# Sparse expert stages in 71 blocks and three phases instead of 78 blocks and two parts, with the prologue's ring copies moved ahead of a root

## Chip, cores and metric

The kernel runs on one core of one Trainium2 chip. The metric is the time of one execution on the device, in microseconds (us); the median of several runs is compared.

## What is computed

The reference is a network of four layers on an input of 8 x 32 x 32 tokens with 64 channels; each layer adds a mixing step (a cosine transform, a convolution, a hyperbolic convolution, a spherical transform) and a feed-forward step to its input, each on normalised rows. The feed-forward steps of the last two layers, called ffn2 and ffn3 in the kernel, are mixtures of 8 experts of which each token takes the best two:

```python
flat = x.reshape(-1, C)                      # 8192 tokens, C = 64, normalised
logits = flat @ router_w.T                   # 8 experts
probs = jax.nn.softmax(logits, axis=-1)
topk_probs, topk_idx = jax.lax.top_k(probs, TOP_K)          # TOP_K = 2
topk_probs = topk_probs / (jnp.sum(topk_probs, axis=-1, keepdims=True) + 1e-09)
gates = jnp.einsum('nk,nke->ne', topk_probs, onehot)
h = jax.nn.silu(einsum('nc,ehc->neh', flat, w1)) * einsum('nc,ehc->neh', flat, w3)   # hidden 682
y = jnp.einsum('neh,ech->nec', h, w2)
out = jnp.einsum('ne,nec->nc', gates, y)
```

## The kernel before

The network's eight stages run one after the other with a barrier between them. The change concerns the two calls of `sparse_stage` (ffn2 and ffn3). The 8192 tokens lie as 64 tiles of 128. Only the two chosen experts are computed for a token: its row is copied to a slot of its expert in DRAM, slots are worked on in blocks of 256 rows of one expert, and results go back to the token's place.

A sparse stage has two programs with a barrier between. The **prologue** normalises the rows in four pieces (`PARTS`: tiles 0 to 7, 8 to 15, 16 to 39, 40 to 63). VectorE centres, sums the squares and scales (`centre`, `variance`, `scale`), ScalarE squares and takes the root (`square`, `take_root`, L1079). TensorE turns the scaled rows (L1033, PSUM tile turn_ps), ScalarE copies them to the tile ring (`keep`, L1088), TensorE multiplies by the router (L1044). VectorE then chooses the two experts (`choose`, from L898), takes the gates, and computes each row's slot (`place`) in two ranges, tiles 0 to 15 and 16 to 63. A first range of 16 tiles lets GpSimd begin early: it stores each tile's rows twice, once per choice, by an indirect DMA (`store_row`, L821), 32 stores in the prologue. `table` (L947 to L970) makes for each range the list of blocks: which expert, which place. SP clears the unfilled end of each expert's region with zero rows (L1019), whose source tile pads VectorE clears (L992).

The **loop** runs over 78 blocks: 23 for the first range and 55 for the second, each 2 x rows / 256 plus 7 spare ones, since each expert's rows of a range begin a block of their own. For each block SP loads the block's 256 rows (x, `load_x`, L1182, 66 KB) and its expert's weights (`load_weights`, L1189, 534 KB), each from a place held in a register; every 13 blocks it loads the registers anew (L1171). Weights have 4 buffers and wait for the down-projection of four blocks earlier; x is issued two blocks ahead of its weights (`X_LEAD`). TensorE turns x (`turn_x`, L1234), ScalarE copies it (L1293), and three pairs of hidden chunks follow: TensorE's up-projection (L1245, 8 matmuls a pair, 24 a block), ScalarE's SiLU (L1303), VectorE's product (L1333). TensorE's order in a block is: up-projection of pairs 0 and 1, turn x of the next block, fold the block before the last, pair 2, down-projection (L1256) of the block before. The trace joins pair 2's successors where they stand together, so a row of 16 up-projection matmuls is the start of a block. VectorE multiplies by the gate (L1321), GpSimd stores the results by two indirect DMAs a block (L1224). Ahead of these stand, on GpSimd, the 96 row stores of the second range. The x of block 23 waits for all of them:

```python
if b == BLOCKS[0]:
    sp.wait_ge(row_stored[1], 16 * 2 * (TILES - SPLIT))
    sp.wait_ge(pads_stored[1], 16 * E)
```

In the **tail** the results are loaded back (L1214), each token's two, and added to X (L1346): tiles 0 to 15 are loaded while the last 13 blocks run, tiles 16 to 63 after the last store, in six pieces of 8 tiles with two loads each.

## Time and profile before

| | |
|---|---|
| three runs | 2366.31, 2366.70, 2370.96 us, median 2366.7 |
| the profiled execution | 2369.53 us, its span 2367.7 us |
| busy in the span | TensorE 74%, VectorE 54%, ScalarE 42%, GpSimd 26% |
| mean granted TensorE clock | 0.842 of 2.4 GHz |
| up-projection matmuls of ffn2 and ffn3 (L1245) | 3744, 491.6 us |
| ffn2: stage start to the loop's start, to the last addition | 1193, 1274, 1712 us |
| ffn3: the loop's start, the last addition | 1919, 2360 us |

A page of the profile shows busy time by engine and in 40 slices of the span, the DMA queues, the chain of work that ended last, and the costliest groups of instructions. A timeline row gives the start in us from the span's start, the duration in us, the engine, the line of the kernel, the operation, what it writes and reads, a count where equal neighbours are joined, and in brackets how long the engine stood idle before it and what ended that. SPq is SP's queue, where only its DMA issues show. The names PE, DVE, ACT and POOL stand for TensorE, VectorE, ScalarE and GpSimd.

### The profile page before, as it was taken

The numbers are of one execution on the slowest core, as the hardware profiler recorded it, in microseconds if no ns is written. First come the engines' busy times: TensorE is split into PE (matmuls) and PEld (weight loads), VectorE is DVE, ScalarE is ACT, GpSimd is POOL, SyncE is SP. The second block draws the span as 40 slices with busy tenths as digits, with TensorE's granted clock in tenths as the row PEclk, the third lists the DMA queues.
The fourth block names the chain that finished last, engine by engine and source line by source line (L and its number), as shares of the span: only waits on it lengthen the run. The fifth ranks groups of instructions, "written<-read, shape, count | busy, mean of one in ns | idle before, by whom it ended". The sixth has DMA issues, their size and how long they took to land. (4 is left out here: it accounts for less than half of the span.)

```text
span 2367.7 us, 31990 instructions
## 1 busy us (share of the span) xinstructions
PE 1756.1 (74%) x11745; PEld 1022.3 (43%) x11745; DVE 1283.6 (54%) x2424; ACT 1000.0 (42%) x1785; POOL 619.5 (26%) x619
## 2 busy tenths in 40 slices
PE   2899996879999942111234999999566449999995
PEld 1633333336333331000022666666356326666663
DVE  6553336665433367688775545555561755455554
ACT  2466653334656532352222444444233324444442
POOL 0100000001000000000035777433351457773332
PEclk8699997996999955555556999999888579999997
DMA  1222210001222100000012544444365134444453
GB/s 49 62 67 63 67 50 20 0 19 55 66 64 70 45 13 0 0 0 0 0 39 85 151 143 142 141 129 156 105 124 110 42 105 143 136 146 134 133 152 133
DMA packets 125790, 187.03 MB, mean 79 GB/s; under 512 B 39194, under 2 KB 73242, under 8 KB 125122
## 3 DMA queue, kind: packets, MB, share of 16 engines
q1 hardware_dynamic: 107458, 166.08, 24.6%
q0 software_dynamic: 18176, 18.91, 2.4%
q8 instruction: 94, 1.54, 0.3%
q14 instruction: 62, 0.51, 0.1%
HBM read 157.26 MB, written 27.65 MB: 78 GB/s over the span
## 5 line engine op out<-in xcount | busy, mean ns | idle before, releaser
L1333 DVE TENSOR_TENSOR ffn_hidden<-ffn_silu,ffn_up_ps 114x512 f32<-114x512 f32 x468 | 321.9, 688 | 397.5 <-ACT ffn_silu L1303 396.6
L1245 PE MATMUL ffn_up_ps<-ffn_turned,ffn_weights 64*114 64x256 f32 x3744 | 491.6, 395 | 20.9 <-DMA ffn_weights<-in_ffn_weights 13.9
L1303 ACT ACTIVATE ffn_silu<-ffn_up_ps 114x512 f32<-114x512 f32 x468 | 279.5, 597 | 445.1 <-PE ffn_up_ps L1245 442.7
L821 POOL DMA_INDIRECT slots<-ffn_rows,ffn_slot x256 | 253.5, 990 | 550.1 <-DVE ffn_slot L938 384.3
L736 ACT ACTIVATE ffn_hidden<-ffn_up_ps,ffn_b 128x512 f32<-128x512 f32 x512 | 310.3, 689 | 198.5 <-PE ffn_up_ps L631 198.5
L1224 POOL DMA_INDIRECT results<-ffn_yout,ffn_xin x312 | 300.4, 963 | 306.3 <-DVE ffn_yout L1321 239.0
L1245 PEld LDWEIGHTS ffn_up_ps<-ffn_turned,ffn_weights 64*114 64x114 f32 x3744 | 318.0, 176 | 136.3 <-issue 80.2
L631 PE MATMUL ffn_up_ps<-ffn_T,ffn_up_w 64*128 64x512 f32 x1024 | 264.5, 630 | 2.2 <-ACT ffn_hidden L736 2.2
L652 PE MATMUL ffn_y_ps<-ffn_hidden,ffn_down 128*64 128x512 f32 x1024 | 247.8, 605 | 2.5 <-DVE ffn_y_total L526 2.5
L1256 PE MATMUL ffn_y_ps<-ffn_hidden,ffn_weights 114*64 114x256 f32 x1872 | 236.4, 388 | 0.0
L526 DVE SCALAR_TENSOR_TENSOR ffn_gated<-ffn_y_ps,ffn_b,ffn_gates 128x512 f32<-128x512 f32 x96 | 72.0, 751 | 204.7 <-PE ffn_y_ps L652 203.1
L631 PEld LDWEIGHTS ffn_up_ps<-ffn_T,ffn_up_w 64*128 64x128 f32 x1024 | 92.9, 190 | 168.8 <-ACT ffn_hidden L736 92.2
L1256 PEld LDWEIGHTS ffn_y_ps<-ffn_hidden,ffn_weights 114*64 114x64 f32 x1872 | 120.5, 136 | 98.8 <-DVE ffn_hidden L1333 52.7
L652 PEld LDWEIGHTS ffn_y_ps<-ffn_hidden,ffn_down 128*64 128x64 f32 x1024 | 62.4, 136 | 160.7 <-ACT ffn_hidden L736 84.4
L1234 PE MATMUL ffn_x_ps<-ident,ffn_xin 128*64 128x128 f32 x312 | 64.6, 289 | 34.2 <-DMA ffn_xin<-slots 34.2
L1267 PE MATMUL ffn_out_ps<-fold,ffn_y_half 128*128 128x64 f32 x624 | 87.8, 264 | 1.4 <-DVE ffn_y_half L1314 1.4
L526 DVE SCALAR_TENSOR_TENSOR ffn_y_total<-ffn_y_ps,ffn_b,ffn_gates 128x512 f32<-128x512 f32 x32 | 23.7, 750 | 115.1 <-PE ffn_y_ps L652 92.0
L1267 PEld LDWEIGHTS ffn_out_ps<-fold,ffn_y_half 128*128 128x128 f32 x624 | 82.4, 192 | 3.2 <-DVE ffn_y_half L1314 1.7
L1033 PE MATMUL ffn_turn_ps<-ident,D 128*128 128x128 f32 x64 | 17.3, 431 | 87.5 <-DVE D L874 87.5
L1314 DVE COPY ffn_y_half<-ffn_y_ps 128x256 f32<-128x256 f32 x156 | 66.3, 425 | 19.8
L1948 POOL MEMSET dc_first<- 128x128 f32 x1 | 0.2, 204 | 288.7 <-POOLq L3081 288.7
L2709 POOL MEMSET hyp_ones<- 128x128 f32 x1 | 0.2, 204 | 288.3 <-POOLq L3081 288.3
(402 smaller groups left out, 2144.7 us busy)
## 6 DMA issues: line engine op xcount, KB each, us to landing
ffn_weights<-in_ffn_weights SPq DMA_DIRECT2D x156, 534.0 KB
ffn_gates<-gate_rows SPq DMA_DIRECT2D x128, 256.0 KB
ffn_xin<-slots SPq DMA_DIRECT2D x156, 66.0 KB, 3.2
sht_mix<-in_sht_weights SPq DMA_DIRECT2D x8, 1024.0 KB, 8.2
results<-ffn_yout,ffn_xin POOLq DMA_INDIRECT x312
slots<-ffn_rows,ffn_slot POOLq DMA_INDIRECT x256
D<-results SPq DMA_DIRECT2D x12, 256.0 KB, 4.8
ffn_second<-results SPq DMA_DIRECT2D x12, 256.0 KB, 5.6
```

What stands on the lines that cost most here:

```text
L526: nc.vector.scalar_tensor_tensor(target, y_ps[th][:, :], b2[:, p:p + 1], gates[:, n % GATES, th, :], ALU.add, ALU.mult).then_inc(y_gated, 1)
L631: nc.tensor.matmul(up_ps[j][:, :], up_w[rows, 2 * p + half, c * P:(c + 1) * P], T[rows, g * NTOK:(g + 1) * NTOK], start=True, stop=True).t ...
L652: last = nc.tensor.matmul(y_ps[th][rows, :], down[:, 2 * p + half, c, :], hidden[:, n % 2 * UNITS + 2 * half + th, :], start=(c == 0), sto ...
L736: nc.scalar.activation(hidden[:, n % 2 * UNITS + j, :], up_ps[j][:, :], ACT.Gelu, bias=b1[:, bias_at:bias_at + 1], scale=1.0).then_inc(hid ...
L821: nc.gpsimd.indirect_dma_start(k.slots, bass.IndirectOffsetOnAxis(slot[c][:, t:t + 1], 0), rows[c][:, t, :], None).then_inc(row_stored[h], 16)
L1224: nc.gpsimd.indirect_dma_start(k.results, bass.IndirectOffsetOnAxis(xin[:, b % HELD, j, CH + 1:CH + 2].bitcast(I32), 0), yout[:, b % HELD, ...
L1245: last = nc.tensor.matmul(up_ps[w][n % 2][0:SIZE, chunk % 2 * BLOCK:(chunk % 2 + 1) * BLOCK], weights[rows_of, b % WEIGHTS, chunk * SIZE:( ...
L1256: last = nc.tensor.matmul(y_ps[b % 2][half * CH:(half + 1) * CH, 0:BLOCK], weights[0:SIZE, b % WEIGHTS, col:col + CH], hidden[0:SIZE, b % ...
L1267: last = nc.tensor.matmul(out_ps[:, j * CH:(j + 1) * CH], y_half[:, b % 2, j * P:(j + 1) * P], k.fold[:, :], start=True, stop=True)
L1303: nc.scalar.activation(silu[0:SIZE, n % 2, :], up_ps[0][n % 2][0:SIZE, :], ACT.Silu).then_inc(silu_done, 1)
L1314: nc.vector.tensor_copy(y_half[:, b % 2, :], y_ps[b % 2][:, 0:BLOCK]).then_inc(y_kept, 1)
L1333: nc.vector.tensor_tensor(hidden[0:SIZE, b % 2, c, :], silu[0:SIZE, n % 2, :], up_ps[1][n % 2][0:SIZE, :], ALU.mult).then_inc(hidden_done, 1)
```

## The change

The second range is split once more for the loop: the blocks come in three phases, 9, 16 and 46, together 71. `LANDED` gives the tiles whose rows must be stored before a phase: 0 to 15, 16 to 31, 32 to 63. Each expert now has one region for all its rows. In the first two phases only blocks that are already full are taken (a count of whole blocks, cut off at 9 and at 16), and the last phase takes all that is left, so that only one partly filled block remains per expert. For this `table` runs three times, keeps a count of the blocks taken (`passed`), and has 17 or 18 operations instead of 13. Unfilled ends are cleared once, after `place(1)`, with a pads tile of half the width. GpSimd's stores are in the same order with two semaphores instead of one. x of a block is issued right behind its weights (only x of block 0 ahead). In the prologue ScalarE's ring copies of the third piece stand ahead of the root of the fourth, and VectorE clears pads behind the scaling of the fourth piece. In the tail all 64 tiles are loaded after the last store, in eight pieces.

```diff
+LANDED = ((0, SPLIT), (SPLIT, 2 * SPLIT), (2 * SPLIT, TILES))
-BLOCKS = tuple(2 * (t1 - t0) * P // BLOCK + SPARES for t0, t1 in RANGES)
+FULL = tuple(2 * t1 * P // BLOCK - SPARES for _, t1 in LANDED[:-1])
+ALL_SLOTS = 2 * TOKENS // BLOCK + SPARES
+PHASES = (FULL[0], FULL[1] - FULL[0], ALL_SLOTS - FULL[1])
+PHASE_AT = (0, FULL[0], FULL[1])
-PADS = 2 * E + 2 * SPARES
+PADS = E + SPARES
...
                 def table(i):
                     ch.link(nc.vector.tensor_reduce(r.blocks[:, :], short, AX.X, ALU.add))
+                    ch.link(nc.vector.tensor_tensor(r.blocks[:, :], r.blocks[:, :], r.passed[:, 0:E], ALU.subtract))
...
+                    ch.link(nc.vector.tensor_scalar(r.starts[:, 1:E + 1], r.starts[:, 1:E + 1], float(nb), None,
+                                                    ALU.min))
+                    ch.link(nc.vector.tensor_tensor(r.taken[:, :], r.starts[:, 1:E + 1], r.starts[:, 0:E],
+                                                    ALU.subtract))
...
                 centre(3)
+                variance(3)
+                scale(3)
                 ch.link(nc.vector.memset(pads[:, :, :, :], 0.0))
                 ch.link(nc.vector.tensor_copy(pads[:, :, :, CH + 1].bitcast(I32), pad_dest), "pads")
-                variance(3)
-                scale(3)
                 table(0)
                 choose(1)
                 gates(1)
                 place(1)
                 table(1)
+                table(2)
...
                 square(3)
+                keep(2)
                 take_root(3)
-                keep(2)
                 keep(3)
...
-            TAIL = 6
+            TAIL = 8
...
                 def load_x(place, b):
                     if b >= HELD:
                         sp.wait_ge(y_stored[b % HELD], 2 * 16 * (b // HELD))
-                    if b == BLOCKS[0]:
-                        sp.wait_ge(row_stored[1], 16 * 2 * (TILES - SPLIT))
-                        sp.wait_ge(pads_stored[1], 16 * E)
+                    if b in PHASE_AT:
+                        i = PHASE_AT.index(b)
+                        sp.wait_ge(row_stored[i], 16 * 2 * (LANDED[i][1] - LANDED[i][0]))
+                    if b == PHASE_AT[-1]:
+                        sp.wait_ge(pads_stored, 16 * E)
+                        sp.wait_ge(spares_stored, 16)
...
-                for b, place in enumerate(registers(block_place, 0, X_LEAD)):
-                    load_x(place, b)
                 for first in range(0, SLOT_BLOCKS, TURN):
-                    experts = registers(block_expert, first, TURN)
-                    places = registers(block_place, first + X_LEAD, min(TURN, SLOT_BLOCKS - first - X_LEAD))
-                    for b in range(first, first + TURN):
+                    count = min(TURN, SLOT_BLOCKS - first)
+                    places, experts = registers(block_place, first, count), registers(block_expert, first, count)
+                    for b in range(first, first + count):
+                        if b == 0:
+                            load_x(places[0], 0)
                         load_weights(experts[b - first], b)
-                        if b + X_LEAD < SLOT_BLOCKS:
-                            load_x(places[b - first], b + X_LEAD)
-                    if first + TURN == SLOT_BLOCKS - TURN:
-                        for b in range(BLOCKS[0]):
-                            sp.wait_ge(y_stored[b], 2 * 16)
-                        for c in (0, 1):
-                            sp.dma_start(back_to[c][:, 0:SPLIT, :], back[c][:, 0:SPLIT, :]).then_inc(first_back, 16)
+                        if b > 0:
+                            load_x(places[b - first], b)
...
-                for t in range(*RANGES[1]):
-                    for c in (0, 1):
-                        store_row(1, c, t)
+                for i in (1, 2):
+                    for t in range(*LANDED[i]):
+                        for c in (0, 1):
+                            store_row(i, c, t)
```

ScalarE in the prologue, from the square of tiles 16 to 39 to the copies of the scaled rows. Before:

```order
L1074 ACTIVATE ffn_second<-D 128x1536
L1079 ACT_TABLE_LOAD
L1079 ACTIVATE ffn_root<-ffn_var,eps_t 128x24
L1074 ACTIVATE ffn_second<-D 128x1536
L1079 ACTIVATE ffn_root<-ffn_var,eps_t 128x24
L1088 COPY ffn_ring<-ffn_turn_ps 128x512 x6
L1094 COPY ffn_rows<-D 128x24x64 x4
```

Now:

```order
L1098 ACTIVATE ffn_second<-D 128x1536
L1103 ACT_TABLE_LOAD
L1103 ACTIVATE ffn_root<-ffn_var,eps_t 128x24
L1098 ACTIVATE ffn_second<-D 128x1536
L1112 COPY ffn_ring<-ffn_turn_ps 128x512 x3
L1103 ACTIVATE ffn_root<-ffn_var,eps_t 128x24
L1112 COPY ffn_ring<-ffn_turn_ps 128x512 x3
L1118 COPY ffn_rows<-D 128x24x64 x4
```

Three of the six ring copies now stand between the second square and the second root.

SP at the start of the loop, from the first register load (TENSOR_LOAD) to the first weights; an ISA row prepares the issue behind it. Before:

```order
L1171 TENSOR_LOAD ffn_block_place
L1182 ISA
L1182 DMA ffn_xin<-slots 128x132
L1182 ISA
L1182 DMA ffn_xin<-slots 128x132
L1171 TENSOR_LOAD ffn_block_expert
L1171 TENSOR_LOAD ffn_block_place
L1189 ISA
L1189 DMA ffn_weights<-in_ffn_weights 128x1068
```

Now, to the x of block 1:

```order
L1192 TENSOR_LOAD ffn_block_place
L1192 TENSOR_LOAD ffn_block_expert
L1206 ISA
L1206 DMA ffn_xin<-slots 128x132
L1213 ISA
L1213 DMA ffn_weights<-in_ffn_weights 128x1068
L1213 ISA
L1213 DMA ffn_weights<-in_ffn_weights 128x1068
L1206 ISA
L1206 DMA ffn_xin<-slots 128x132
```

Both register loads stand first, x of block 0 is the only one ahead of weights, and x of block 1 stands behind the weights of block 1.

VectorE in the prologue, the third and fourth piece between `place(0)` and the first table. Before:

```order
L874 TENSOR_TENSOR D<-D,ffn_rstd 128x1536
L860 TENSOR_REDUCE ffn_mean<-X 128x24
L861 SCALAR_TENSOR_TENSOR D<-ffn_mean,X 128x1536
L992 MEMSET ffn_pads 128x3960
L993 CAST ffn_pads<-ffn_consts 128x60
L868 TENSOR_REDUCE ffn_var<-ffn_second 128x24
L873 RECIPROCAL ffn_rstd<-ffn_root 128x24
L874 TENSOR_TENSOR D<-D,ffn_rstd 128x1536
L947 TENSOR_SCALAR ffn_count<-ffn_count 128x8
L948 TENSOR_TENSOR ffn_wide<-ffn_consts,ffn_count 128x64
```

Now:

```order
L865 TENSOR_REDUCE ffn_mean<-X 128x24
L866 SCALAR_TENSOR_TENSOR D<-ffn_mean,X 128x1536
L873 TENSOR_REDUCE ffn_var<-ffn_second 128x24
L878 RECIPROCAL ffn_rstd<-ffn_root 128x24
L879 TENSOR_TENSOR D<-D,ffn_rstd 128x1536
L1020 MEMSET ffn_pads 128x1980
L1021 CAST ffn_pads<-ffn_consts 128x30
L960 TENSOR_SCALAR ffn_counts<-ffn_counts 128x8
L961 TENSOR_TENSOR ffn_wide<-ffn_consts,ffn_counts 128x64
L965 TENSOR_REDUCE ffn_blocks<-ffn_wide 128x8
```

The clearing of pads, 1980 columns instead of 3960, now stands behind the scaling of D and ahead of the first table.

## Rows read from the trace of the kernel before

**Rows 1.** TensorE, loop of ffn2: start us, us, engine line op out<-in xcount [idle].

```profile
1302.95 0.41 PE L1234 MATMUL ffn_x_ps<-ident,ffn_xin 128*64 128x128 f32 x2
...
1401.32 1.99 PE L1245 MATMUL ffn_up_ps<-ffn_turned,ffn_weights 64*114 64x256 f32 x16 [2.43 <-issue]
...
1684.37 1.99 PE L1245 MATMUL ffn_up_ps<-ffn_turned,ffn_weights 64*114 64x256 f32 x16
```

**Rows 2.** Stretches: us, busy of PE, PEld, DVE, ACT, POOL, PEclk, DMA share, GB/s.

```profile
2041.00:2054.00 13.00, 9.24 (x56) 6.16 (x54) 3.72 (x7) 2.72 (x6) 9.95 (x11) 0.74 0.51 173
1404.00:1684.00 280.00, 280.00 (x2287) 187.47 (x2288) 146.39 (x273) 131.05 (x273) 136.47 (x143) 1.00 0.44 139
1703.00:1708.00 5.00, 0.00 (x0) 0.00 (x0) 3.84 (x6) 0.00 (x0) 0.00 (x0) 0.50 0.95 332
```

**Rows 3.** TensorE's timeline, the pause in ffn3's loop.

```profile
2045.80 3.76 PE L1245 MATMUL ffn_up_ps<-ffn_turned,ffn_weights 64*114 64x256 f32 x16 [3.76 <-issue]
...
2053.63 1.99 PE L1245 MATMUL ffn_up_ps<-ffn_turned,ffn_weights 64*114 64x256 f32 x16
```

**Rows 4.** SP's queue, loads in the loops of ffn2 and ffn3.

```profile
1296.65 0.33 SPq L1182 DMA_DIRECT2D ffn_xin<-slots  x1
...
1344.47 0.50 SPq L1182 DMA_DIRECT2D ffn_xin<-slots  x1
...
1397.09 0.33 SPq L1182 DMA_DIRECT2D ffn_xin<-slots  x1
...
1944.95 0.40 SPq L1182 DMA_DIRECT2D ffn_xin<-slots  x1
...
2041.68 0.33 SPq L1182 DMA_DIRECT2D ffn_xin<-slots  x1
```

**Rows 5.** VectorE's timeline, prologue of ffn2.

```profile
1226.36 3.36 DVE L992 MEMSET ffn_pads<- 128x3960 f32 x1 [0.89 <-DVE D L861]
...
1234.48 0.17 DVE L947 TENSOR_SCALAR ffn_count<-ffn_count 128x8 f32<-128x8 f32 x1
...
1247.89 0.75 DVE L898 COPY ffn_L<-ffn_small_ps 128x192 f32<-128x192 f32 x2 [9.59 <-PE ffn_small_ps L1044]
...
1268.08 0.17 DVE L947 TENSOR_SCALAR ffn_count<-ffn_count 128x8 f32<-128x8 f32 x1
...
1273.40 0.19 DVE L970 CAST ffn_block_place<-ffn_place_f 128x55 int32<-128x55 f32 x1
```

**Rows 6.** SP's queue, then TensorE's timeline, start of ffn2's loop.

```profile
1274.80 0.91 SPq L1182 DMA_DIRECT2D ffn_xin<-slots  x2
1279.71 0.34 SPq L1189 DMA_DIRECT2D ffn_weights<-in_ffn_weights  x1
...
1284.38 3.76 PE L1245 MATMUL ffn_up_ps<-ffn_turned,ffn_weights 64*114 64x256 f32 x16 [7.05 <-DMA ffn_weights<-in_ffn_weights]
```

**Rows 7.** VectorE's timeline, ffn2's tail; then the chain that ended last, ffn3's.

```profile
1711.55 0.69 DVE L1346 TENSOR_TENSOR X<-X,ffn_second 128x512 f32<-128x512 f32 x1
...
2351.74 6.35 DMA ffn_second<-results
```

**Rows 8.** GpSimd's timeline, ffn2: the loop's 32nd row store.

```profile
1313.91 0.96 POOL L821 DMA_INDIRECT slots<-ffn_rows,ffn_slot  x1 [0.31 <-issue]
```

**Rows 9.** Loads of the input tile in ffn2, all 78: time to landing.

```profile
DMA to landing us min/median/max: 3.0/3.2/3.8
```

**Rows 10.** ScalarE's, then TensorE's timeline, prologue of ffn2.

```profile
1225.51 1.48 ACT L1074 ACTIVATE ffn_second<-D 128x1536 f32<-128x1536 f32 x1 [5.81 <-DVE D L861]
1231.93 0.31 ACT L1079 ACTIVATE ffn_root<-ffn_var,eps_t 128x24 f32<-128x24 f32 x1 [4.94 <-DVE ffn_var L868]
1232.15 1.05 ACT L1088 COPY ffn_ring<-ffn_turn_ps 128x512 f32<-128x512 f32 x2
1235.73 0.59 ACT L1088 COPY ffn_ring<-ffn_turn_ps 128x512 f32<-128x512 f32 x1 [2.53 <-PE ffn_turn_ps L1033]
...
1237.44 1.11 PE L1033 MATMUL ffn_turn_ps<-ident,D 128*128 128x128 f32 x4
```

122 lines of the change are left out of this document (62 added, 60 removed).

## The prediction

> **What bounds the kernel now.** From the page (the table above) I took only that TensorE leads and where its clock is full. Then I read its timeline inside a block loop. From block 22 to block 77 of ffn2 the up-projections of one block start one period after those of the block before: (1684.37 - 1401.32) / 55 = 5.146 us [rows 1], and over 1404 to 1684 us TensorE is busy in all of the 280 us at granted clock 1.00, the 2.4 GHz level [rows 2]. So in the loop a block costs what TensorE needs for it, and a block less is 5.146 us less. The weights are read anew for each block and no instruction depends on how full a block is, so an empty block costs the same.
>
> Three places around that loop are not TensorE's. First, block 22: its up-projections start 2.43 us late in ffn2 [rows 1], and 3.76 us late in ffn3 [rows 3]. SP's queue says why: x of block 23, the first of the second part, is issued in front of the weights of block 22, and SP issues it only at 1397.09 (ffn3: 2041.68) [rows 4], when GpSimd has stored the rows of all 48 remaining tiles. In ffn3 the first 16 matmuls after the pause take 3.76 instead of 1.99 us, and the granted clock is 0.74 over 2041 to 2054, part of it at the 1.2 GHz level [rows 2]: block 22 lasts 2053.63 - 2045.80 = 7.83 us, 2.7 more than a period. The wait costs 2.4 us in ffn2 and 3.8 + 2.7 = 6.4 us in ffn3. Second, the start: VectorE ends the last table at 1273.6 [rows 5], SP issues its first load at 1274.80 and the first weights at 1279.71, and TensorE's first up-projection, held by those weights, comes 4.67 us later [rows 6]. Third, the tail: after the last block the results of tiles 16 to 63 come back and are added pair by pair until 1712.2 [rows 7].
>
> **The change, part by part.** The durations are those of the profiled execution, 2369.5 us (span 2367.7); the median of the three runs, 2366.7, lies 2.8 us lower, and the sum is put on the median at the end.
>
> *Blocks.* 78 becomes 71 in each stage: 7 x 5.146 = 36.0 us, twice: -72.0 us. They come off the full-clock part, where no other engine could have hidden them.
>
> *The wait at block 22.* It goes, and two later waits could take its place: x of block 9 wants the rows of tiles 16 to 31, x of block 25 those of tiles 32 to 63. Each now stands behind the weights of its own block. The slot behind the weights of block 4 is 1296.65 and then one per period [rows 4], so x of block 9 is due at 1322.4 and of block 25 at 1404.7. GpSimd's stores come 0.96 + 0.30 = 1.26 us apart, and the 32nd of the loop starts at 1313.91 [rows 8]; 64 stores before SP's release at 1397.09 is 1316.4, 2.5 us after that start. So the rows are there 6.0 and 7.6 us early. In ffn3 the slot of block 5 is 1944.95 [rows 4]: 1965.5 against 2041.68 - 80.6 = 1961.1, and 2047.9 against 2041.7, so 4.4 and 6.2 us. Loop and stores start from the same barrier; SP's earlier start (below) takes 0.9 us off each margin, which leaves at least 3.5 us. Behind such a wait on SP stand the weights of the next block, due a period later, and TensorE stops only if x comes over 3 us too late on top (next edit). So neither wait stops TensorE: -2.4 - 6.4 = -8.8 us; bounds: nothing gained if the wait only moves, and all of it.
>
> *Input loads.* x was issued two blocks ahead; now x of block b follows the weights of block b, which wait for the down-projection of block b - 4. The old slot behind the weights of block 4 is 1296.65 [rows 4], and TensorE turns the rows of block 4 at 1302.95 [rows 1]: 6.3 us. x lands 3.0 to 3.8 us after its issue in all 78 loads of ffn2 [rows 9], nearly all of them issued right behind a weight load, as now. That leaves 2.5 us. At every 13th block SP reloads its registers: the slot due at 1296.65 + 9 x 5.146 = 1342.96 came at 1344.47 [rows 4], 1.5 us late, and there 1.0 us is left. Cost nothing; bounds nothing and about 10 us (ten such blocks by 1 us).
>
> *Prologue.* On ScalarE the three ring copies of tiles 16 to 39 move ahead of the root of tiles 40 to 63. They waited behind that root until 1232.15; now they start when the square ends, at 1227.0, and the third, 3.6 us after the first as before, ends at 1231.2. The root starts there instead of at 1231.93, the scaling ends 2.55 us later as before, at 1233.7 instead of 1234.5, and TensorE's next transposes, which stood at 1237.44 behind the late copies, start at once [rows 5, 10]. The steps after them run as before, so the router's logits come 3.7 us earlier and VectorE's second choice starts at 1244.2 instead of 1247.89. The clearing of the padding moves behind that scaling at half the width, half of 3.36 us; with the first table it ends near 1240, inside VectorE's wait of 9.59 us before that choice [rows 5]. Without that cover it would cost its 1.7 us.
> Against this stand the tables. The old one behind the choice took 1268.08 to 1273.59, 5.5 us for 13 operations of 8 to 440 columns; the old first one, from 1234.48 until that wait began at 1238.30, 3.8 us for 13 of 8 to 184 [rows 5]. Now two follow the choice: 18 operations of 8 to 128 columns, at most 3.8 + 5 x 0.2 = 4.8, and 17 of 8 to 368, about 5.1 + 4 x 0.2 = 5.9 (a small operation is 0.17 us, about 0.2 with the step to the next); with one more small operation 10.9 us. That is 5.4 more, minus the 3.7: the loop may begin 1.7 us later. SP gives some back: the load of x of block 1 and a short register load, 0.9 us together by my estimate from the two loads' 0.91 us at 1274.80 and the 1.2 us before it [rows 5, 6], no longer stand ahead of the first weights; x of block 0 now runs beside those weights (66 KB, 0.2 us at the 332 GB/s below). Net +1.0 us a stage, +2.0; bounds -1 and +4 a stage.
>
> *Tail.* The first 16 tiles came back early; now 8 pairs of 256 KB loads instead of 6 follow the last store. VectorE's two additions of a pair, 0.69 us each [rows 7], are 2.8 us for two more pairs if the data is there; 2 x 0.52 MB at the 332 GB/s of 1703 to 1708 us, with the DMA engines 0.95 busy, are 3.2 us [rows 2]. In ffn3 the chain ends on a transfer that took 6.35 us [rows 7], so there the DMA decides. I take 3.0 us a stage, +6.0; bounds 2.4 (a quarter faster transfers) and 6 a stage.
> The Trainium skill (DMA: Bandwidth & Descriptors, Specifications) gives a fabric ceiling of 435 GB/s; at that the extra 1.05 MB would be an estimated 2.4 us a stage, hidden by VectorE's additions, and the sum 0.4 us lower. The row with engines 0.95 busy at 332 GB/s does not bear that out for these transfers.
>
> Sum: -72.0 - 8.8 + 2.0 + 6.0 = -72.8 us. On the profiled execution that is 2296.7, on the median 2366.7 - 72.8 = 2293.9, say **2294 us**.
>
> **The rivals.**
> *The wait moves.* The new boundaries wait as the old one did. For it: the margin of block 9 in ffn3 is 3.5 us, and if GpSimd is slowed, all 32 stores grow. Against it: the pitch of 1.26 us fits the 64 stores after the 32nd as well. TensorE would stop once the 32 stores took 6 us (15%) longer. Each wait then costs 2.4 to 6.4 us as before, two to four of them: 2299 to 2320, most likely two by 5, 2304.
> *Reload blocks wait.* x misses its turn at the ten blocks after a register reload, by 1 us each: 2304.
> *The lead is too short everywhere* (the other side). If x, now just in time, landed later than 6.3 us after its issue, each block would wait: every 0.1 us costs 142 x 0.1 = 14 us, and from 6.8 us on the change is slower than before; at 7.0 us it would stand at 2294 + 99 = 2393. Against it: none of 78 took over 3.8 us beside weights and stores.
> *The blocks were free.* If the seven blocks cost nothing, being spare ones without rows, only -8.8 + 8.0 remains, 2366. Against it: 55 periods in a row of one length, the last ones among them.
>
> **How the numbers follow.** 0.84 for the forecast, 0.08 for the moved wait, 0.05 for the reload blocks, 0.02 for the short lead, 0.01 for free blocks. 0.2% (4.7 us) is about what a measurement of this kernel can tell from no change. Faster: 0.84 + 0.08 + 0.05 = 0.97; same 0.01; slower 0.02. Range: downwards the prologue's bound gives 4 and the tail's 1.2, and the runs shown scatter by 2 about their middle: 2287. Upwards the bounds of prologue and tail give 6 each: 2306, and 1 for the rest; that takes in most of the two middle rivals: 2307.
>
> **What would show it.** 24 x 142 = 3408 up-projection matmuls; period 5.15; no pause over 1 us in the loops and clock 1.00 throughout them once it has risen; SP's x of blocks 9 and 25 right behind the weights; VectorE's second choice 3.7 us earlier and its last table 1.7 us later than now, against the stage's start; from the last result store to the last addition 3 us more. A period above 5.2, or pauses at blocks 9, 25, 13 or 26, would make me wrong.

## The result, and the profile after

The changed kernel takes 2288.97 us (median of four executions, 2279.4 to 2290.99) where the kernel before, on the same chip, took 2366.51: a ratio of 0.966, 95% interval 0.9631 to 0.969. Repeated on another occasion it was 2286.04 against 2368.84, ratio 0.9645 (0.9618 to 0.9672). The forecast was 2294, range 2287 to 2307. The direction and the bulk are right; the gain is larger than forecast (-77.5 us, in the repetition -82.8, where -72.8 was predicted), and 0.966 x 2366.7 = 2286.2 us lies below the range.

The profiled execution of the changed kernel is the 2279.4 one (span 2277.6), 9.6 us under its median. So the two spans, 90.1 us apart, may not be compared as wholes: 10 us of it lie in the first dense stage, which the change does not touch (last section). I compare the two sparse stages piece by piece, each piece from a start inside the stage. The stage starts are SP's first issue of the router weights: 1193.05 and 1838.88 us before, 1186.64 and 1790.15 after. The last piece ends at SP's first issue of the next stage, in ffn3 at its issue of the network's output.

| us | forecast, ffn2 / ffn3 | ffn2: before, after, difference | ffn3: before, after, difference |
|---|---|---|---|
| stage start to first up-projection | +1.0 / +1.0 | 91.33, 89.55, **-1.78** | 89.85, 88.67, **-1.18** |
| first up-projection to start of last result store | -38.4 / -42.4 | 412.41, 372.82, **-39.59** | 415.22, 371.99, **-43.23** |
| start of last result store to next stage's start | +3.0 / +3.0 | 16.99, 19.70, **+2.71** | 17.11, 20.10, **+2.99** |
| sum | -34.4 / -38.4 | -38.66 | -41.42 |

The sparse stages together gave -80.1 instead of -72.8: of the 7.3 us more, 5.0 are in the first row and 2.0 in the second. The tail is right within 0.3. In the repetition's profile the same pieces, against the same profile before, give -78.4: 5.6 us more than forecast, 4.7 of them in the first row and 0.9 in the second, with the tail right within 0.1. So the first row's miss repeats; of the second row's, half is no more than two profiles of one kernel differ by.

The loop first. The page's row of the up-projections and the stretches of both loops after the clock has risen:

```profile
L1262 PE MATMUL ffn_up_ps<-ffn_turned,ffn_weights 64*114 64x256 f32 x3408 | 445.8, 394 | 5.8 <-DMA ffn_weights<-in_ffn_weights 4.9
```

```profile
1290.00:1640.00 350.00, 350.00 (x2858) 234.25 (x2857) 182.90 (x340) 163.62 (x341) 206.80 (x216) 1.00 0.46 139
1892.00:2240.00 348.00, 348.00 (x2842) 232.88 (x2844) 182.13 (x339) 162.29 (x338) 206.82 (x217) 1.00 0.46 139
```

3408 matmuls instead of 3744, as counted, TensorE busy in every microsecond at granted clock 1.00, the 2.4 GHz level; the last column and the one before are GB/s and DMA share, 139 as before [rows 2] and 0.46 for 0.44. The pause that stood in [rows 1, 3] is nowhere: each gating multiplication of VectorE follows the one before by 5.14 or 5.15 us in both stages, but for the last two gaps, which are shorter. SP's queue in ffn2 shows why the new boundaries don't wait, with GpSimd's 32nd and 96th row store of the loop beside it:

```profile
1313.44 0.33 SPq L1213 DMA_DIRECT2D ffn_weights<-in_ffn_weights  x1
1313.96 0.33 SPq L1206 DMA_DIRECT2D ffn_xin<-slots  x1
...
1395.79 0.33 SPq L1213 DMA_DIRECT2D ffn_weights<-in_ffn_weights  x1
1396.37 0.33 SPq L1206 DMA_DIRECT2D ffn_xin<-slots  x1
```

```profile
1308.90 0.96 POOL L826 DMA_INDIRECT slots<-ffn_rows,ffn_slot  x1 [0.31 <-issue]
...
1389.72 0.95 POOL L826 DMA_INDIRECT slots<-ffn_rows,ffn_slot  x1 [0.30 <-issue]
```

Before, SP issued x of block 23 2.37 us after the start of the 96th store (to 1397.09 [rows 4]):

```profile
1394.72 0.95 POOL L821 DMA_INDIRECT slots<-ffn_rows,ffn_slot  x1 [0.30 <-issue]
```

By that, the rows of block 9 are there at 1308.90 + 2.37 = 1311.3 and those of block 25 at 1392.1: 2.7 and 4.3 us before their loads, which stand 0.5 us behind the weights like every other. The same reckoning gives 2.0 and 3.6 us in ffn3.

Now the first row of the table. VectorE's prologue in ffn2, after:

```profile
1220.53 1.75 DVE L873 TENSOR_REDUCE ffn_var<-ffn_second 128x24 f32<-128x1536 f32 x1 [1.62 <-ACT ffn_second L1098]
...
1227.39 1.71 DVE L1020 MEMSET ffn_pads<- 128x1980 f32 x1 [0.48 <-DVE D L879]
...
1237.42 0.75 DVE L903 COPY ffn_L<-ffn_small_ps 128x192 f32<-128x192 f32 x2 [3.81 <-PE ffn_small_ps L1068]
...
1257.86 0.17 DVE L960 TENSOR_SCALAR ffn_counts<-ffn_counts 128x8 f32<-128x8 f32 x1
...
1268.42 0.19 DVE L992 CAST ffn_block_place<-ffn_place_f 128x46 int32<-128x46 f32 x1
```

Against its stage's start the second choice (the copy of the logits) stood at 1247.89 - 1193.05 = 54.84 us [rows 5] and stands at 50.78: 4.06 earlier, 3.7 forecast. The two tables behind the choice take 1268.61 - 1257.86 = 10.75, forecast 10.9. So the last table ends 81.97 us after the start instead of 80.54: +1.43, forecast +1.7. Up to here the sum holds. It breaks in SP's queue:

```profile
1271.24 0.37 SPq L1206 DMA_DIRECT2D ffn_xin<-slots  x1
1271.79 0.88 SPq L1213 DMA_DIRECT2D ffn_weights<-in_ffn_weights  x2
```

```profile
L1192 SPq TENSOR_LOAD <-ffn_block_place x1: 987/987/987, 1269.1 to 1269.1; - x1
L1192 SPq TENSOR_LOAD <-ffn_block_expert x1: 964/964/964, 1270.1 to 1270.1; - x1
```

From the end of the last table to the first weights it was 1279.71 - 1273.59 = 6.12 us [rows 5, 6] and is 1271.79 - 1268.61 = 3.18: 2.94 less (ffn3: 2.96), where I had taken 0.9. The second pair of lines (loads of the table into SP's registers: ns shortest/median/longest, and their start) shows two loads of 13 registers in about 1.0 us each. The same view of the kernel before, at the same place, has three: 476 ns for two registers, 1023 for the 13 experts, and 2731 for 13 places.

```profile
L1171 SPq TENSOR_LOAD <-ffn_block_place x2: 476/1604/2731, 1274.2 to 1276.8; - x2
L1171 SPq TENSOR_LOAD <-ffn_block_expert x1: 1023/1023/1023, 1275.8 to 1275.8; - x1
```

TensorE's first up-projection follows the first weights by 4.40 us, where it was 4.67 [rows 6]:

```profile
1276.19 3.76 PE L1262 MATMUL ffn_up_ps<-ffn_turned,ffn_weights 64*114 64x256 f32 x16 [2.48 <-DMA ffn_weights<-in_ffn_weights]
```

And the second row: it is -36.0 for the blocks and -2.4 (ffn2) for the pause, and 1.2 more (ffn3: 0.8 more). Before, one of the last four result stores takes 1.79 us instead of 0.96 (GpSimd's and VectorE's timeline, end of ffn2 before; then GpSimd's after):

```profile
1693.17 1.22 DVE L1346 TENSOR_TENSOR X<-X,D 128x1024 f32<-128x1024 f32 x1
1693.42 1.79 POOL L1224 DMA_INDIRECT results<-ffn_yout,ffn_xin  x1 [0.31 <-issue]
1694.42 1.23 DVE L1346 TENSOR_TENSOR X<-X,ffn_second 128x1024 f32<-128x1024 f32 x1
...
1695.52 0.96 POOL L1224 DMA_INDIRECT results<-ffn_yout,ffn_xin  x1 [0.30 <-issue]
```

```profile
1646.48 0.96 POOL L1241 DMA_INDIRECT results<-ffn_yout,ffn_xin  x1 [0.30 <-issue]
1647.74 0.96 POOL L1241 DMA_INDIRECT results<-ffn_yout,ffn_xin  x1 [0.30 <-issue]
1649.01 0.96 POOL L1241 DMA_INDIRECT results<-ffn_yout,ffn_xin  x1 [0.30 <-issue]
```

The long store of before starts while VectorE makes the early addition of tiles 0 to 15, and ends 0.82 us after the end of that addition's first operation. Without the early addition none of these stores is long. Those 0.83 us a stage were not in my sum.

The tail. The chain that ended last, in ffn3 after:

```profile
2254.78 5.10 DMA ffn_second<-results
2260.63 1.31 DVE X L1363 x2
```

Behind that transfer VectorE's additions follow one another to the end; before, the chain went through a transfer of 6.35 us instead [rows 7]. So the tail is now bound by the additions: four more of 0.69 us, 2.8 us, where I had let the transfers' 3.2 us decide and taken 3.0.

### The profile page after: what moved, and what is told of

The parts are those of the page before. It is cut to its first block and busy times, and to the rows that moved or that the text cites. A ratio compares the mean times of both kernels' runs of the same rounds, so it can differ in the third digit from the quotient of the medians.

```text
span 2277.6 us, 30440 instructions
## 1 busy us (share of the span) xinstructions
PE 1677.3 (74%) x11157; PEld 967.5 (42%) x11157; DVE 1245.0 (55%) x2416; ACT 965.8 (42%) x1715; POOL 590.1 (26%) x591
## 5 line engine op out<-in xcount | busy, mean ns | idle before, releaser
L1350 DVE TENSOR_TENSOR ffn_hidden<-ffn_silu,ffn_up_ps 114x512 f32<-114x512 f32 x426 | 293.0, 688 | 349.9 <-ACT ffn_silu L1320 349.0
L1262 PE MATMUL ffn_up_ps<-ffn_turned,ffn_weights 64*114 64x256 f32 x3408 | 445.8, 394 | 5.8 <-DMA ffn_weights<-in_ffn_weights 4.9
L1320 ACT ACTIVATE ffn_silu<-ffn_up_ps 114x512 f32<-114x512 f32 x426 | 254.4, 597 | 388.9 <-PE ffn_up_ps L1262 386.5
L1241 POOL DMA_INDIRECT results<-ffn_yout,ffn_xin x284 | 271.9, 957 | 246.0 <-DVE ffn_yout L1338 179.6
L1262 PEld LDWEIGHTS ffn_up_ps<-ffn_turned,ffn_weights 64*114 64x114 f32 x3408 | 288.1, 176 | 110.6 <-issue 59.6
L1273 PE MATMUL ffn_y_ps<-ffn_hidden,ffn_weights 114*64 114x256 f32 x1704 | 215.2, 388 | 0.0
L1273 PEld LDWEIGHTS ffn_y_ps<-ffn_hidden,ffn_weights 114*64 114x64 f32 x1704 | 109.7, 136 | 89.9 <-DVE ffn_hidden L1350 48.2
L1284 PE MATMUL ffn_out_ps<-fold,ffn_y_half 128*128 128x64 f32 x568 | 79.7, 263 | 1.4 <-DVE ffn_y_half L1331 1.4
L2138 PE MATMUL dc_conv_ps<-dc_fresh,dc_step_w 128*128 128x512 f32 x144 | 67.6, 617 | 8.8 <-DVE dc_fresh L2124 8.8
L1310 ACT COPY ffn_turned<-ffn_x_ps 64x256 f32<-64x256 f32 x142 | 50.1, 353 | 56.0 <-PE ffn_x_ps L1251 56.0
```

Source lines behind the costliest of these rows:

```text
L1241: nc.gpsimd.indirect_dma_start(k.results, bass.IndirectOffsetOnAxis(xin[:, b % HELD, j, CH + 1:CH + 2].bitcast(I32), 0), yout[:, b % HELD, ...
L1262: last = nc.tensor.matmul(up_ps[w][n % 2][0:SIZE, chunk % 2 * BLOCK:(chunk % 2 + 1) * BLOCK], weights[rows_of, b % WEIGHTS, chunk * SIZE:( ...
L1273: last = nc.tensor.matmul(y_ps[b % 2][half * CH:(half + 1) * CH, 0:BLOCK], weights[0:SIZE, b % WEIGHTS, col:col + CH], hidden[0:SIZE, b % ...
L1284: last = nc.tensor.matmul(out_ps[:, j * CH:(j + 1) * CH], y_half[:, b % 2, j * P:(j + 1) * P], k.fold[:, :], start=True, stop=True)
L1320: nc.scalar.activation(silu[0:SIZE, n % 2, :], up_ps[0][n % 2][0:SIZE, :], ACT.Silu).then_inc(silu_done, 1)
L1350: nc.vector.tensor_tensor(hidden[0:SIZE, b % 2, c, :], silu[0:SIZE, n % 2, :], up_ps[1][n % 2][0:SIZE, :], ALU.mult).then_inc(hidden_done, 1)
```

## The experiments

Two theories stood for the 5 us of the prologue: that a register load is quick or slow by **where its first entry lies** (every slow one of both traces starts at an entry that is no multiple of four, that is not on 16 bytes, every quick one of 13 on one: before, places from entry 2, 15 and 41 took 2.7, from entry 28 0.98), or by **what was issued ahead of it** (before, two row transfers). Two runs set one against the other.

Six of the runs of this section are single executions: the old table moved, the new tables moved, the early addition moved, both orders undone, cleared twice, and the kernel before with the copies ahead. Their whole times tell little, and what is read from them lies inside a stage.

**The old table moved to 16 bytes.**

```
-block_place = sb("block_place", [P, SLOT_BLOCKS], I32)
+block_place = sb("block_place", [P, SLOT_BLOCKS + 2], I32)   # entries from column 2 on
-registers(block_place, first + X_LEAD, ...)
+registers(block_place, first + X_LEAD + 2, ...)
```

> The kernel before, with one edit: the table of block places lies two entries further in its tile, so that the load of places 2 to 14 into SP's registers begins at a multiple of four entries (16 bytes) instead of at entry 2. Same loads, same transfers, same order. Theory (a register load is quick, 75 ns a register, where its first entry lies on 16 bytes, and slow, 205 ns a register, elsewhere): that load at the start of each sparse stage's loop takes 1.0 us instead of 2.73, the first weights are issued 1.75 us earlier, and each stage is 1.75 us shorter, 3.5 in all; the later loads of places turn quick where they start at entries 15, 28, 41 ... plus 2 = 4 entries' multiples and slow elsewhere. Rival (the load is slow because two transfers of rows were issued just ahead of it, or because of where its instructions lie): it stays at 2.7 us and no stage changes.

The load takes 989 ns, with the two row transfers still ahead of it:

```profile
L1172 SPq TENSOR_LOAD <-ffn_block_place x1: 989/989/989, 1278.2 to 1278.2; - x1
```

The first up-projection comes 89.01 and 87.86 us after the stage's start instead of 91.33 and 89.85: 2.3 and 2.0 earlier. But the stages did not get shorter (start to last addition 521.9 and 519.9 us; before 519.2 and 520.7), and the time is 2368.71 us beside 2369.51. The second half of the expectation is a miss. TensorE's timeline in ffn2's loop shows where the two microseconds went, and more:

```profile
1403.30 3.76 PE L1246 MATMUL ffn_up_ps<-ffn_turned,ffn_weights 64*114 64x256 f32 x16 [5.93 <-issue]
```

Block 22 now waits 5.93 us where it waited 2.43 [rows 1], in ffn3 6.31 where it waited 3.76 [rows 3]. GpSimd's stores did not start sooner, and in both stages SP issues x of block 23 2.37 us after the 96th of them, as before. Part of the growth is scatter: in the run with the moved addition (below), whose start is that of the kernel before, the two pauses are 4.41 and 2.12 us. But there too the pause is long where the loop was early: in ffn2 the first gating multiplication came 104.40 us after the stage's start, where it was 106.11 before and is 103.25 here; in ffn3 105.54, 103.42 and 101.42. Pause and start add up to 108.5 to 109.2 us in ffn2 and 107.2 to 107.7 in ffn3 in all three traces. Whatever the loop gains at its start, that pause takes back; and behind a long pause the first matmuls take 3.76 instead of 1.99 us, as in [rows 3]. So in the kernel before, the quick load is worth nothing; it is worth its 2 us only together with the pause's removal.

**The new tables moved off 16 bytes.**

```
-mine = slice(PHASE_AT[i], PHASE_AT[i] + nb)
+mine = slice(PHASE_AT[i] + 1, PHASE_AT[i] + nb + 1)
-table[0:1, bass.ds(first, count)]
+table[0:1, bass.ds(first + 1, count)]
```

> The changed kernel, with one edit: both block tables lie one entry further in their tiles, so that SP's two first loads of 13 registers begin at entry 1 instead of entry 0. Theory (a load whose first entry is not on 16 bytes takes 205 ns a register instead of 75): both take 2.7 us instead of 0.98 and 0.96, the first weights come 3.4 us later after VectorE's last table, and since no wait further on takes it up, each sparse stage ends 3.4 us later, 6.9 in all: the old kernel's slow start is back. Of the later loads, begun at entries 14, 27, 40, 53 and 66, none is quick (in the changed kernel the pair at entry 52 was). Rival (the changed kernel's first loads are quick because no transfer was issued ahead of them): they stay below 1.1 us.

```profile
L1192 SPq TENSOR_LOAD <-ffn_block_place x1: 2732/2732/2732, 1276.2 to 1276.2; - x1
L1192 SPq TENSOR_LOAD <-ffn_block_expert x1: 2698/2698/2698, 1278.9 to 1278.9; - x1
...
L1192 SPq TENSOR_LOAD <-ffn_block_place x1: 1052/1052/1052, 1474.5 to 1474.5; - x1
L1192 SPq TENSOR_LOAD <-ffn_block_expert x1: 968/968/968, 1475.6 to 1475.6; - x1
```

Both first loads are slow again, with no transfer ahead of them. I had written that no later load would be quick; the pair at 1474.5 is, and it starts at entry 39 + 1 = 40, a multiple of four that I had overlooked. The rule, not my list, was right. The first up-projection comes 93.84 and 91.56 us after the start; in the unedited kernel of the repetition 89.50 and 88.99: 4.3 and 2.6 later, 6.9 together. The two stages are 5.5 us longer to their last addition (485.2 and 481.8 against 481.1 and 480.4), and the time is 2293.64 us beside 2363.43.

**The lead of the rows taken away in the kernel before.**

```
-for b, place in enumerate(registers(block_place, 0, X_LEAD)):
-    load_x(place, b)
...
+if b == 0: load_x(places[0], 0)
 load_weights(experts[b - first], b)
-if b + X_LEAD < SLOT_BLOCKS: load_x(places[b - first], b + X_LEAD)
+if b > 0: load_x(places[b - first], b)
```

> The kernel before, with one edit: the lead of the rows over the weights is taken away, so that the rows of a block are asked for right behind its weights (rows of block 0 ahead of them), as in the changed kernel. 78 blocks, two phases, and the early add stay. Theory: the row transfer that waits for the second phase's stores (block 23) now stands two weight loads further back, 10.3 us later, so the pause of TensorE at block 22 goes in both stages (2.4 and 6.4 us); the place table's first load starts at entry 0 and takes 1.0 us instead of 0.48 + 2.73, so the first weights come some 2 to 2.9 us earlier a stage; in all -8.8 and -4 to -6, 2352 to 2354 us against 2366.5. Rival 1 (the pause was bound to the number of stores, not to the lead): a pause of 2 us or more remains at block 22 or 23 and the time is over 2358. Rival 2 (rows asked for so late are late at every block): the period of 5.146 us grows, and the time is above 2366.

2358.05 us against 2369.51, ratio 0.9958 (0.9944 to 0.9972): 9.9 us less by the ratio and 11.5 by the medians, where 13 to 15 were expected. The register loads behaved (0.98 and 0.97 us), the first up-projection came 2.9 and 2.1 us earlier, and the period stayed 5.146, so rows asked for right behind the weights are not late; only once, behind a reload of the registers in ffn3, did TensorE wait for rows (0.39 us). But the pause did not go, it shrank to about 1.5 us in each stage. It now stands at the transposes of block 23's rows, with SP's row ahead of it:

```profile
1398.50 0.33 SPq L1181 DMA_DIRECT2D ffn_xin<-slots  x1
```

```profile
1400.47 0.41 PE L1233 MATMUL ffn_x_ps<-ident,ffn_xin 128*64 128x128 f32 x2 [1.42 <-DMA ffn_xin<-slots]
```

So the smaller lead was not the whole cure: what freed the changed kernel is that and the boundary, which moved from block 23 to 25, 10.3 us later on TensorE, for the same 96 stores. Rival 1 is half right.

**The early addition moved behind the first tail transfer, in the kernel before.**

```
-dve.wait_ge(first_back, 32)
-add(0, SPLIT)
 for i, (t0, t1) in enumerate(tail):
     dve.wait_ge(tail_back[i], 32)
+    if i == 0: dve.wait_ge(first_back, 32); add(0, SPLIT)
     add(t0, t1)
```

> The kernel before, with one edit: the adds of tiles 0 to 15 wait for the first tail transfer, so they no longer run beside the last four result stores. Everything is still computed. Theory (the add of two SBUF operands on VectorE holds up GpSimd's store beside it): all of the last four stores of each sparse stage take 0.96 us, none 1.79, and the last store comes 0.83 us earlier after its up-projections than before; the two adds (1.2 us each) then lie in VectorE's idle time between the tail pieces, so each stage is about 0.8 us shorter, 1.7 in all. Rival (the long store is late for another reason, its own transfer queue for example): one store of 1.79 us stays, and nothing is earlier. Second rival: the adds push the tail's own adds back, and a stage becomes up to 2.5 - 0.8 = 1.7 us longer although the store is short.

```profile
1694.22 0.96 POOL L1224 DMA_INDIRECT results<-ffn_yout,ffn_xin  x1 [0.30 <-issue]
1695.48 0.96 POOL L1224 DMA_INDIRECT results<-ffn_yout,ffn_xin  x1 [0.30 <-issue]
1696.75 0.96 POOL L1224 DMA_INDIRECT results<-ffn_yout,ffn_xin  x1 [0.30 <-issue]
```

In both stages all of the last stores are short. So the addition beside it is what made one long. Three stores of ffn2's prologue before begin within an operation of VectorE of 1.76 us on two operands in SBUF, and each ends 0.83 us after that operation does. The longest of them:

```profile
1232.68 1.76 DVE L874 TENSOR_TENSOR D<-D,ffn_rstd 128x1536 f32<-128x1536 f32 x1
1232.91 2.36 POOL L821 DMA_INDIRECT slots<-ffn_rows,ffn_slot  x1 [0.30 <-issue]
```

The additions did not fit in idle time, though: from the last store to the last addition it is 16.7 and 16.9 us instead of 15.5 and 15.6, so the stage loses 1.2 and gains 0.83: the second rival, smaller than its bound. The whole, 2368.34 beside 2369.51, tells nothing here.

The Trainium skill (SBUF — State Buffer, "SBUF: two separate sides") says that a VectorE operation with two SBUF inputs and a GpSimd operation that reads SBUF exclude each other for a whole instruction. That fits the rows of 1.79 and 2.36 us for the stores, which end 0.82 and 0.83 us after VectorE's operation, much as if they had only begun there. The trace does not show it for VectorE: its next operation on two SBUF operands starts at 1694.42 and takes its usual 1.23 us beside the rest of the store. The prediction did not draw on this page.

**The prologue's two moves.** Three edits of the changed kernel and one of the kernel before price them; the measure is the second choice's distance from the stage's start in ffn2 (54.84 before, 50.78 after, 50.79 in the repetition).

```
 keep(2) / take_root(3)      ->  take_root(3) / keep(2)                     (root ahead)
 the same, and pads' memset  ->  ahead of variance(3)                       (both orders undone)
 the same, and the memset    ->  twice                                      (cleared twice)
 kernel before: take_root(3) / keep(2)  ->  keep(2) / take_root(3)          (copies ahead)
```

> The changed kernel, with one part undone: ScalarE takes the root of the last part (tiles 40 to 63) ahead of the copies of the third part's turned rows, as before. Theory: the wait of those copies for the root puts the turned products of tiles 16 to 39 back, the second choice starts 3 to 4 us later, and the loop with it: 3 to 4 us a stage, 6 to 8 in all (0.3%). Rival 1 (it is the later clearing of the pads that brings the second choice forward, and the order on ScalarE alone does nothing): within 1 us. Rival 2 (VectorE is the bound of this stretch, and an earlier root lets it scale the last part sooner): 1 to 3 us a stage faster.

> The changed kernel, with both moves of the prologue undone, the padding still cleared at half the old width: ScalarE takes the last part's root ahead of the copies, and VectorE clears the padding ahead of the last part's variance. With the root alone moved back the second choice came 0.9 us later (51.66 against 50.78 us after the stage's start). Theory: VectorE waits 1.6 us for ScalarE's square at that place, and the half-width clearing (1.71 + 0.20 us with its gaps) fills that wait and overhangs by 0.4 us: the second choice comes 0.9 + 0.4 = 1.3 us later than in the changed kernel, at 52.1 us, and 2.7 us earlier than in the kernel before. So most of the 4.06 us is not in the order but in the halved width. Rival (the order of the clearing carries the gain, as the prediction put it): the second choice is back at 54 us or later.

> The same, with the half-width clearing done twice, so that VectorE is held as long as by the old full-width one (2 x 1.71 us): the old prologue with the new tables. Theory: the overhang grows by 1.75 us and goes straight through root, copies and turned products: the second choice comes 1.3 + 1.75 = 3.0 us later than in the changed kernel (53.8 us after the stage's start), the last table and the loop as much. Rival (the second choice is bound elsewhere, by the products of the last part): less than 2 us later.

> The kernel before, with the one move on ScalarE alone: the copies of the third part's turned rows ahead of the last part's root; the padding is cleared in its old place at its old width (3.36 us). Theory (as the prediction put it, the copies' wait for that root is what held the second choice back): the second choice comes 2.5 to 3.7 us earlier, at 51.1 to 52.3 us after the stage's start instead of 54.84, and the last table and GpSimd's stores as much earlier; the loop's pause at block 22 is bound to those stores, so the stage ends as much earlier. Rival (the clearing must go too, because it delays the last part's scaling and with it the last transposes): the second choice moves by less than 1.5 us.

The copy of the logits in VectorE's timeline, of root ahead, both undone, cleared twice, and of the kernel before with the copies ahead:

```profile
1244.79 0.36 DVE L903 COPY ffn_L<-ffn_small_ps 128x192 f32<-128x192 f32 x1 [6.75 <-PE ffn_small_ps L1068]
```

```profile
1247.12 0.75 DVE L903 COPY ffn_L<-ffn_small_ps 128x192 f32<-128x192 f32 x2 [9.15 <-PE ffn_small_ps L1068]
```

```profile
1249.71 0.36 DVE L903 COPY ffn_L<-ffn_small_ps 128x192 f32<-128x192 f32 x1 [9.16 <-PE ffn_small_ps L1069]
```

```profile
1242.41 0.75 DVE L898 COPY ffn_L<-ffn_small_ps 128x192 f32<-128x192 f32 x2 [6.63 <-PE ffn_small_ps L1044]
```

Minus the stage starts (1193.13, 1194.66, 1195.03, 1190.50) these are 51.66, 52.46, 54.68 and 51.91 us. So from the changed kernel backwards: the root ahead costs 0.9 (3 to 4 was expected: a miss), the clearing ahead 0.8 more, a clearing as long as the old one 2.2 more, and that is the old prologue, 3.9 later. From the kernel before forwards the copies alone give 2.9 of the 4.1. Halving the clearing is then worth 2.2 to 2.4 us by itself (54.68 or 54.84 to 52.46). There is no contradiction: what was late is the chain clearing, variance, root, copies. It can be shortened by taking the clearing out of it or by going round the root, and either edit gives most of what both give. The time of root ahead, 2291.1 against 2369.51 (ratio 0.9684, 0.9663 to 0.9705), does not differ measurably from the changed kernel's, nor do its stages (481.5 and 479.8 us against 481.1 and 480.4 in the repetition). With both orders undone it took 2290.14, with the clearing twice 2297.01, beside 2363.43 for the kernel before. The kernel before with the copies ahead took 2357.53 beside 2367.28: there GpSimd's stores start sooner too, so both stages end earlier in spite of the pause (517.6 and 516.4 us).

**The changed kernel again.**

> The changed kernel itself, unedited, to compare the next run with on the same chip, and to see how much the stages that the change does not touch vary. Theory: ratio to the kernel before 0.966 to 0.968; both sparse stages within 1.5 us of 480.5 and 479.2 us; the first dense stage, 298.4 us in the one profile so far and 308.6 in that of the kernel before, comes back near 306 to 309 us, with a granted clock near 0.92, because nothing in it was changed. Rival (something of the change reaches that stage): it is again below 300 us.

Ratio and sparse stages (481.1, 480.4 us) are as expected. The first dense stage took 305.7 us, near the 308.6 of the kernel before: nothing of the change is in it.

**A version that beats both.** The expectations above leave one large item: the two tables at the prologue's end, 10.75 us in which, but for SP's padding stores, only VectorE works; and only the blocks from 9 on need them. This kernel makes them in the loop's program instead:

```
-place(1); table(1); table(2)          # prologue
+place(1)                              # prologue
...
+table(1); table(2)                    # VectorE, ahead of its first product of the loop
...
-for first in range(0, SLOT_BLOCKS, TURN):
+for first, end in ((0, 9), (9, 17), (17, 25), (25, 38), (38, 51), (51, 64), (64, 71)):
+    if first in PHASE_AT[1:]: sp.wait_ge(late, LATE[PHASE_AT.index(first) - 1])
...
+    if b == WEIGHTS - 1:              # the padding rows of the experts, once in the prologue
```

> The changed kernel, with the second and third tables taken out of the prologue: VectorE makes them at the start of the block loop, while SP loads the first rows and weights; the padding rows of the experts are stored by SP after the loads of blocks 0 to 3, and SP loads the registers of blocks 0 to 8 first. Theory: the prologue ends after the second placing, 10.7 us earlier; the two tables take 10.75 us of VectorE, which had 10.3 us to wait there for the first product, and of the first loads' register time 0.6 us a stage goes too; the first product then waits about 1.5 us for VectorE; net 9 to 10 us a stage, 18 to 20 in all, ratio to the kernel before 0.958. Rival 1 (the tables' operations of two SBUF operands hold up GpSimd's row stores beside them, block 9's rows come too late and TensorE pauses there): a pause of 1 to 5 us at block 8 or 9, net 5 to 9 us a stage. Rival 2 (GpSimd's queue is the end of the prologue, not VectorE): the barrier moves by less than 2 us, and so does the time.

2267.49 us against 2368.84, ratio 0.9575 (0.9554 to 0.9595); the changed kernel beside it 2286.04. That is another 18.55 us less. VectorE's rows from the first operation of the loop's program to the first products, and TensorE's first up-projection:

```profile
1264.36 0.17 DVE L836 TENSOR_SCALAR ffn_counts<-ffn_counts 128x8 f32<-128x8 f32 x1 [0.54 <-PEq L876]
...
1274.99 0.19 DVE L868 CAST ffn_block_place<-ffn_place_f 128x46 int32<-128x46 f32 x1
1275.21 1.28 DVE L1357 TENSOR_TENSOR ffn_hidden<-ffn_silu,ffn_up_ps 114x512 f32<-114x512 f32 x2
```

```profile
1271.12 3.76 PE L1265 MATMUL ffn_up_ps<-ffn_turned,ffn_weights 64*114 64x256 f32 x16 [2.24 <-DMA ffn_weights<-in_ffn_weights]
```

The first up-projection comes 78.48 us after the start instead of 89.50, and the first product waits until 1275.21 where ScalarE had its operand at 1273.82: 1.4 us. TensorE in turn waits for the products, 0.50 us here and 1.39 in ffn3. GpSimd's stores beside the tables kept their 0.96 us but for one in each stage (1.12 and 1.11). No pause came at block 8 or 9.

A last run tried to take those 1.4 us as well, by one table operation behind each product, and by the first weights ahead of the first rows:

```
-table(1); table(2)
+table(1); then, behind each product of the first blocks, one operation of table(2)
...
-places, experts = registers(...), registers(...); load_x(places[0], 0); load_weights(experts[0], 0)
+experts = registers(...); load_weights(experts[0], 0); places = registers(...); load_x(places[0], 0)
```

> The run with the two later tables in the block loop, with two more edits: the third table's 17 operations are spread over the first six blocks, one behind each product, instead of lying ahead of the first; and SP issues the first weights after one register load, ahead of the second register load and the first rows. Theory: the first product no longer waits 1.4 us for VectorE, and the first up-projection comes 0.8 to 1.3 us earlier; VectorE has 2 us of each 5.15 us period to spare, so the spread operations delay nothing; each sparse stage is 2 to 2.7 us shorter than with both tables ahead, 4 to 5.4 in all, ratio to the kernel before 0.9555. Rival (each operation behind a product delays the next product, and TensorE waits for it): the first six periods grow by 0.3 us or more each, and the gain is under 2 us in all.

2268.64 against 2367.28, ratio 0.9589 (0.9573 to 0.9604): no gain over the run before. The first product no longer waits, but the first up-projection does, 0.95 us longer (79.43 us after the start). SP's and TensorE's timelines:

```profile
1268.47 0.36 SPq L1226 DMA_DIRECT2D ffn_weights<-in_ffn_weights  x1
1269.80 0.34 SPq L1219 DMA_DIRECT2D ffn_xin<-slots  x1
```

```profile
1273.68 0.63 PE L1277 MATMUL ffn_x_ps<-ident,ffn_xin 128*64 128x128 f32 x2 [15.49 <-DMA ffn_xin<-slots]
```

The first rows are turned 3.9 us after their issue here, behind the weights; in the run before, ahead of the weights, 2.0 us (1266.24 to 1268.24). So the edit's two halves about cancelled: to their last addition the two stages took 470.6 and 469.2 us, in the run before 471.7 and 468.9. Which half cost and which gained was not tried one by one.

## Why the prediction was right, and where it failed

*Blocks, -72.0.* Right: 3408 matmuls, a period of 5.146 us, clock 1.00.

*The wait at block 22, -8.8, and no new one.* Right in the sum: no pause in either loop. The margins were smaller than worked out (in ffn2 2.7 and 4.3 us, not 5.1 and 6.7; in ffn3 2.0 and 3.6, not 3.5 and 5.3), and the pause is a poorer number than I took it for. SP's issue at its end comes 2.37 us after the start of the 96th store, whenever the loop starts, so the pause grows by what is saved ahead of it: by the gaps between VectorE's gating multiplications the two stages' pauses, with the low clock behind them, cost 16 us in the run with the table on 16 bytes, 9.0 in the kernel before, and 10.5 in the run with the moved addition, which starts like it. Taking it as a term beside the prologue's was right only because the pause and the prologue's delay vanish together.

*Prologue, +1.0 a stage.* This is **the step that failed**: "SP gives some back: the load of x of block 1 and a short register load, 0.9 us together". It gave back 2.94 us. I let the two 13-register loads stand at what they took before, without a row for either; one of them was slow because it began at entry 2 of its table. With the lead of two blocks that start went too, and the load fell from 2.73 to 0.99 us. The bound of -1 a stage should have come from that gap of 4.0 us between SP's rows at 1274.80 and 1279.71 [rows 6], most of which I left unexplained. In ffn2 the first up-projection also followed the first weights 0.3 us sooner, where I had added 0.2; in ffn3 it came 0.2 later, as I had it. The other two terms held: the second choice 4.06 earlier for 3.7, the tables 5.2 us longer for 5.4. That the first of them held is partly luck. Its mechanism, the copies' wait for the root, gives 2.9 by itself in the kernel before and only 0.9 in the changed kernel; the rest is the clearing, which I thought off the path and which stood at its head.

*Tail, +3.0 a stage.* +2.71 and +2.99. It now ends on VectorE's additions, not on the transfers as I had it.

*Not in the sum:* the early addition that held up one result store, 0.83 us a stage, 1.7 in all.

5.0 from the prologue, 1.7 from the store, and smaller differences of under 0.5 each, are the 7.3 us between -72.8 and -80.1; in the repetition's profile it is 4.7 from the prologue out of 5.6. The medians show -77.5 and -82.8 on the two occasions; the untouched stages, which vary by more than these differences, are in them too. None of the rivals came true.

## What to carry to other kernels

A wait that is set by another engine's end takes back whatever is saved ahead of it: before pricing an edit, ask which of the later waits moves with it, and take the two terms together. Where the trace shows a gap between two issues of a queue, find a row for each part of it, register loads included, before taking any of it as fixed. And where one engine works alone at a program's start, ask which of its results the first iterations need: the rest can be made beside the first loads.

## What was not expected of the hardware

- **A load of SP's registers from a table in SBUF** takes 0.96 to 1.05 us for 13 where its first entry is a multiple of four (16 bytes from the table's start), 2.67 to 2.81 us elsewhere. Every load of 13 in ffn2 of both kernels and of the two runs with shifted tables falls on its side. The 75 ns a register that this makes is no price of a register, though. In the run with the tables in the loop 7 registers from entry 64 took as long as 13:

```profile
L1186 SPq TENSOR_LOAD <-ffn_block_place x1: 957/957/957, 1588.4 to 1588.4; - x1
```

There 9 from entry 0 took 0.75 us and 8 from entry 0 of another table 0.53, but 8 from entries 9 and 17 took 1.69 to 1.74; before, 2 from entry 0 took 0.48. These durations fit steps of 0.21 to 0.27 us each: one step for four entries together where the load begins at a multiple of four, and one for every entry left over, or for every entry where it begins elsewhere. That makes 4 steps for 13 or 7 registers, 3 for 9, 2 for 8 or 2, and 13 for 13 that begin elsewhere. Two loads, each the first after a wait, took 0.2 us more (9 in 0.96, 8 in 0.74). That reading is worked out from the durations alone; no run was made for it, and why a load goes this way stays open.

- **One store of GpSimd took 1.79 us instead of 0.96** beside an addition of VectorE of 128x1024 on two SBUF operands, and 0.96 without it. In the prologue of ffn2 before, the three stores that began within operations of 1.76 us on two SBUF operands took 1.68 to 2.36 us. Beside short operations less is at stake: in the prologues the stores that grew beside operations of 0.56 us took up to 1.34, and beside the tables' operations in the loop (0.17 to 0.78 us) one store of a stage grew, to 1.12.
- **A stage that nothing had changed** took 308.6 us before, 298.4 in the profile after and 305.7 in the repetition. Its granted clock went with it (stretch 52 to 340 us: us, TensorE, its weight loads, VectorE, ScalarE, GpSimd, clock, DMA share, GB/s; before, after, repetition):

```profile
52.00:340.00 288.00, 274.14 (x1206) 113.68 (x1208) 120.86 (x231) 163.34 (x271) 8.27 (x8) 0.92 0.23 65
```

```profile
52.00:340.00 288.00, 272.52 (x1248) 107.27 (x1250) 125.32 (x238) 169.22 (x280) 8.30 (x9) 0.96 0.23 66
```

```profile
52.00:340.00 288.00, 274.01 (x1228) 110.99 (x1228) 122.79 (x235) 166.46 (x276) 8.28 (x8) 0.94 0.23 66
```

In the same 288 us TensorE made 1206, 1248 and 1228 matmuls, at clocks of 0.92, 0.96 and 0.94. What set the clock in that stage stays open. It is the reason why differences of a few us are read here inside a stage, not from the whole.
